# Mixing weights summed pair by pair, and five smaller moves around the attention-to-experts handover

## What is computed

```
x = x + xattn(layernorm(x), ctx, ctx)          # 16 heads of 16, rope, row q sees keys q-64 .. q
z = layernorm(x).reshape(1600, 256)
logits = z @ router_w.T                        # 8 experts
topk_p, topk_i = top_k(softmax(logits), 2); topk_p /= topk_p.sum(-1)
for e in range(8):
    sel = topk_i == e; mask = sel.any(-1)
    mean_w = (topk_p * sel).sum() / max(mask.sum(), 1)      # one number for each expert
    h = silu(z @ gate_w[e].T) * (z @ up_w[e].T)             # 1024 wide
    out += mask[:, None] * (h @ down_w[e].T) * mean_w
x = x + out
```

## Time and profile before

| | us |
|---|---|
| median of 3 runs (range) | 498.06 (497.79 to 502.31) |
| profiled execution | 498.84 |
| its span, first to last instruction | 497.0 |
| PE busy | 448.1 (90%) |
| DVE busy | 301.9 (61%) |
| ACT busy | 271.8 (55%) |
| POOL busy | 125.0 (25%) |
| mean granted TensorE clock | 0.962 |

### The profile page before, as it was taken

How to read it: one execution, slowest core, us unless ns; L and a number is a source line. 1 busy time by engine, 2 the same in 40 slices (tenths; PEclk the granted TensorE clock), 3 DMA queues, 4 the chain that set the end, 5 groups by cost and what they waited for, 6 DMA issues and landing times.

```text
span 497.0 us, 8914 instructions
## 1 busy us (share of the span) xinstructions
PE 448.1 (90%) x2788; PEld 371.4 (75%) x2788; DVE 301.9 (61%) x728; ACT 271.8 (55%) x855; POOL 125.0 (25%) x129
## 2 busy tenths in 40 slices
...
GB/s 236 30 245 119 167 23 42 30 65 8 63 10 59 21 47 52 56 241 226 176 191 54 162 155 135 176 103 164 154 131 171 103 169 125 37 31 39 9 2 36
...
## 3 DMA queue, kind: packets, MB, share of 16 engines
...
...
## 4 chain that ended last, share of the span: by engine, by line
PE 70%; ACT 8%; DVE 8%; issue 5%; POOL 3%; DMA 3%; SPq 2%; ACTq 1%; POOLq 0%; DVEq 0%
PE b_o L694 8%; PE b_small L694 8%; PE b_s L681 7%; PE b_s L683 7%; PE b_s L682 7%; PE b_s L442 6%; ACT probs L814 4%; PE b_pv L465 3%; PE b_pt L451 3%; PE b_proj L520 2%; PE b_pt L681 2%; PE b_pt L682 2%; PE b_pt L683 2%; PE b_s L440 2%; PE b_o L540 2%
## 5 line engine op out<-in xcount | busy, mean ns | idle before, releaser
L814 ACT ACTIVATE probs<-b_s,negmax 100x100 f32<-100x100 f32 x256 | 85.8, 361 | 21.9 <-DVE negmax L1092 18.9
L1302 POOL DMA_INDIRECT out<-y_sb,idnow x32 | 49.7, 1552 | 159.8 <-ACT y_sb L854 152.5
L842 ACT CAST h_hi<-h_sb 128x448 fp32r<-128x448 f32 x64 | 36.3, 567 | 87.6 <-DVE h_sb L1169 87.6
L681 PE MATMUL b_s<-x_hi,w_hi 128*128 128x448 f32 x192 | 72.0, 375 | 0.0
L683 PE MATMUL b_s<-x_hi,w_lo 128*128 128x448 f32 x192 | 70.9, 369 | 0.0
L682 PE MATMUL b_s<-x_lo,w_hi 128*128 128x448 f32 x192 | 70.6, 368 | 0.0
L1070 DVE TENSOR_TENSOR w_lo<-w_raw,w_hi 128x1024 fp32r<-128x1024 f32 x48 | 58.8, 1224 | 13.8 <-ACT w_hi L777 13.8
L1173 DVE TENSOR_TENSOR h_lo<-h_sb,h_hi 128x448 fp32r<-128x448 f32 x64 | 40.0, 625 | 40.5 <-ACT h_hi L842 40.5
L814 ACT ACTIVATION_READ_ACCUMULATOR probs<-b_s,negmax 100x1 f32 x256 | 56.8, 222 | 0.0
L442 PE MATMUL b_s<-kblk,qrot 128*100 128x400 f32 x128 | 53.6, 499 | 0.0
L1092 DVE TENSOR_REDUCE negmax<-b_s 100x4 f32<-100x400 f32 x64 | 36.2, 566 | 24.5 <-PE b_s L442 23.9
...
## 6 DMA issues: line engine op xcount, KB each, us to landing
...
kblk<-krot SPq DMA_DIRECT2D x128, 12.5 KB, 1.8
...
```

The lines of the kernel that those rows point to most:

```text
L681: pe.matmul(o, wh[:, c, cols], x_hi[:, c, :], start=(c == 0), stop=False)
L814: m = nc.scalar.activation(probs[:, N % 3, h, :], b_s[N % 3][0:S, h * S:(h + 1) * S], ACT.Exp, bias=negmax[:, N % 4, h:h + 1], accum_out=p ...
L842: nc.scalar.copy(h_hi[:, f, :], h_sb[:, f % 2, :]).then_inc(s_hhi, 1)
L1302: G.indirect_dma_start(out, bass.IndirectOffsetOnAxis(idnow[:, n:n + 1], 0), y_sb[:, n, :], None, bounds_check=TOK + TILE - 1, oob_is_err= ...
```

## The change

- `weight_sums` works on one pair: DVE's differences, ACT's exponentials and POOL's sums of pair i-2 are made in round i, and POOL adds them into `wacc`. On POOL the sums of pairs 6 and 7 stand ahead of the second half of `scatter(6)` and of `scatter(7)`; the first half of `scatter(6)` stands between them. PE waits for the eighth sum (`s_wpair`).
- The pad rows of tile 0 and the slot numbers are sent behind the key blocks of pair 2; the tail of expert e+1 is written one load earlier than before, and the tails count on two semaphores in turn.
- `early_tile` is made of transposes in place of plain products, and six `warm` matmuls are added around it and around `route_logits(6)`, with one more ahead of it.
- ACT applies SiLU to one number between `x_high(0)` and the reloads, so the table of SiLU is loaded there.
- `take_ids(0)` stands at step 3 (`FC - 5`) of tile 0 in place of step 5.

Left out of the diff: semaphores and buffers that are only renamed.

```diff
@@ -145,12 +145,13 @@
         topi = sb("topi", [S, 2, E], U32)
         choice = sb("choice", [S, TOPK, 2])
         sel = sb("sel", [S, NPAIR, TOPK * 2, E])
-        delta = sb("delta", [S, TOPK, B])
-        etop = sb("etop", [S, TOPK, B])
-        esum = sb("esum", [S, B])
-        erec = sb("erec", [S, B])
-        wtop = sb("wtop", [S, TOPK, B])
-        wsel = sb("wsel", [S, NPAIR, TOPK * 2, E])
+        delta = sb("delta", [S, 2, TOPK, 2])
+        etop = sb("etop", [S, 2, TOPK, 2])
+        esum = sb("esum", [S, 2])
+        erec = sb("erec", [S, 2])
+        wtop = sb("wtop", [S, TOPK, 2])
+        wsel = sb("wsel", [S, TOPK * 2, E])
+        whalf = sb("whalf", [S, 2, E])
         chosen = sb("chosen", [S, 2, E], BF16)
         before = sb("before", [S, 3, E], BF16)
         place = sb("place", [S, 2, E])
@@ -159,6 +160,7 @@
         desti = sb("desti", [S, 2, TOPK * 2], U32)
         wacc = sb("wacc", [S, E])
         credit = sb("credit", [1, 4])
+        table = sb("table", [1, 1])
 
         cnt = sb("cnt", [P, E])
         cnt1 = sb("cnt1", [P, E])
@@ -368,11 +369,12 @@
             sp.wait_ge(s_zero, 3)
             key_blocks(0)
             load_rows(2, 2, NPAIR)
-            sp.dma_start(slots[0:TILE, :], padrows).then_inc(s_pre, 16)
-            sp.dma_start(slot_sb[:, :], slotno).then_inc(s_slot, 16)
             for i in pairs:
                 if i + 1 < NPAIR:
                     key_blocks(i + 1)
+                if i == 1:
+                    sp.dma_start(slots[0:TILE, :], padrows).then_inc(s_pre, 16)
+                    sp.dma_start(slot_sb[:, :], slotno).then_inc(s_slot, 16)
                 if i >= 1:
                     store_x2(i - 1)
             for q in s_scat:
@@ -386,10 +388,11 @@
                 n = sp.value_load(counti[0:1, e:e + 1], min_val=0, max_val=TOK)
                 row = nc.s_assert_within(n + e * REGION, 0, E * REGION - TILE)
                 sp.dma_start(slots[bass.ds(row, TILE), :].rearrange("(p g) w -> p (g w)", g=GRP),
-                             padrows.rearrange("(p g) w -> p (g w)", g=GRP)).then_inc(s_tails, 16)
+                             padrows.rearrange("(p g) w -> p (g w)", g=GRP)).then_inc(s_tails[e % 2], 16)
 
             sp.wait_ge(s_tail, 1)
             write_tail(0)
+            write_tail(1)
             sp.wait_ge(s_first, 1)
             for e in range(E):
                 lo = sp.value_load(first[0:1, e:e + 1], min_val=0, max_val=MAXTILES)
@@ -398,7 +401,7 @@
                     for q in s_scat:
                         sp.wait_ge(q, 16 * TOPK * 2 * (NPAIR // 2))
                     sp.wait_ge(s_xt[DC - 1], 2)
-                sp.wait_ge(s_tails, 16 * (e + 1))
+                sp.wait_ge(s_tails[e % 2], 16 * (e // 2 + 1))
                 with sp.Fori(lo, hi) as t:
                     sp.wait_ge(s_xt[DC - 1], t + 1)
                     sp.wait_ge(s_id, t + 1)
@@ -406,8 +409,8 @@
                     sp.dma_start(xin[:, :, :].rearrange("p g w -> p (g w)"),
                                  slots[bass.ds(row, TILE), :].rearrange("(p g) w -> p (g w)", g=GRP)
                                  ).then_inc(s_in, 16)
-                if e + 1 < E:
-                    write_tail(e + 1)
+                if e + 2 < E:
+                    write_tail(e + 2)
             total = sp.value_load(first[0:1, E:E + 1], min_val=1, max_val=MAXTILES)
             taken = sp.to_reg(total + 1)
             sp.wait_ge(s_xt[DC - 1], taken)
@@ -585,7 +588,8 @@
                 for c in range(DC):
                     for g in range(GRP):
                         pe.matmul(b_xt[c][:, g * ROWS:(g + 1) * ROWS], xin[:, g, c * P:(c + 1) * P],
-                                  ident[0:ROWS, 0:ROWS], start=(g == 0), stop=False, skip_group_check=True)
+                                  ident[0:ROWS, 0:ROWS], is_transpose=True, start=(g == 0), stop=False,
+                                  skip_group_check=True)
 
             def late_rows(i):
                 last = i == NPAIR - 1
@@ -614,8 +618,9 @@
                     if cur:
                         scores(i, n)
                     if n == 5 and i == NPAIR:
-                        warm(4)
+                        warm(5)
                         early_tile()
+                        warm(3)
                     if n == 5 and 0 <= i - 2 < NPAIR:
                         ranks(i - 2)
                     if n == 2 and prv:
@@ -644,8 +649,12 @@
                         o_project(2 * i - 1)
                     if n % 4 in (0, 1) and 0 <= N - 3 < NQ * NPAIR:
                         values(N - 3)
+                    if n == 2 and i == NPAIR:
+                        warm(2)
                     if n == 2 and 0 <= i - 2 < NPAIR:
                         route_logits(i - 2)
+                    if n == 2 and i == NPAIR:
+                        warm(1)
                     if n == 2 and i == NPAIR + 1:
                         late_rows(NPAIR - 2)
 
@@ -656,7 +665,7 @@
                       start=True, stop=True).then_inc(s_cnt, 1)
             warm(4)
             late_rows(NPAIR - 1)
-            pe.wait_ge(s_wacc, 1)
+            pe.wait_ge(s_wpair, NPAIR)
             pe.matmul(b_o[:, 0:E], cst[0:S, C_ONE:C_ONE + P], wacc[:, :],
                       start=True, stop=True).then_inc(s_wsum, 1)
 
@@ -767,6 +776,12 @@
                 nc.scalar.copy(xn2T[:, :, :, :].rearrange("p b c s -> p (b c s)"),
                                b_small[:, 0:DC * PT]).then_inc(s_x2Tc, 1)
 
+            def top_exponentials(i):
+                a.wait_ge(s_dl, i + 1)
+                if i >= 2:
+                    a.wait_ge(s_wpair, i - 1)
+                nc.scalar.activation(etop[:, i % 2], delta[:, i % 2], ACT.Exp).then_inc(s_et, 1)
+
             def rows_high(i):
                 a.wait_ge(s_xr, i + 1)
                 nc.scalar.copy(xr_hi[:, i % 2], xrow[:, i % 2, :, 0:D]).then_inc(s_xrh, 1)
@@ -792,6 +807,8 @@
                             a.wait_ge(s_pv, M - 2)
                         nc.scalar.copy(probsT[:, M % 3].rearrange("p h s -> p (h s)"),
                                        b_pt[0:S, 0:QH * S]).then_inc(s_pTc, 1)
+                    if n == 5 and 0 <= i - 2 < NPAIR:
+                        top_exponentials(i - 2)
                     if n == 1 and i == NPAIR:
                         rows_high(NPAIR - 2)
                     if n == 0 and i == NPAIR + 1:
@@ -825,8 +842,6 @@
                         evac_proj(i + 1, 0, s_q, s_qc)
 
 
-            a.wait_ge(s_dl, 1)
-            nc.scalar.activation(etop[:, :, :], delta[:, :, :], ACT.Exp).then_inc(s_et, 1)
 
             def x_high(t):
                 for c in range(DC):
@@ -883,6 +898,7 @@
                     step(t, e, par, False, False)
 
             x_high(0)
+            nc.scalar.activation(table[:, :], cst[0:1, C_ONE:C_ONE + 1], ACT.Silu)
             for k in range(WCH):
                 reload(-1, k)
             a.wait_ge(s_first, 1)
@@ -1058,11 +1074,11 @@
                     V.tensor_tensor(onehot[:, b, :], slot_sb[:, :], bc(here[:, b:b + 1], [S, TILE]), ALU.is_equal
                                     ).then_inc(s_hot, 1)
 
-            def top_differences():
-                V.tensor_tensor(delta[:, :, :].rearrange("p k t -> p t k"),
-                                top[:, :, :, 0:TOPK].rearrange("p i b k -> p (i b) k"),
-                                bc(top[:, :, :, 0:1].rearrange("p i b k -> p (i b) k"), [S, B, TOPK]),
-                                ALU.subtract).then_inc(s_dl, 1)
+            def top_differences(i):
+                if i >= 2:
+                    v.wait_ge(s_et, i - 1)
+                V.tensor_tensor(delta[:, i % 2].rearrange("p k b -> p b k"), top[:, i, :, 0:TOPK],
+                                bc(top[:, i, :, 0:1], [S, 2, TOPK]), ALU.subtract).then_inc(s_dl, 1)
 
             def weights_low(e, par, k):
                 v.wait_ge(s_whi, WCH * (e + 1) + k + 1)
@@ -1115,8 +1131,8 @@
                         residual(i - 1)
                     if n == 3 and 0 <= i - 2 < NPAIR:
                         choose_counts(i - 2)
-                    if n == 3 and i == NPAIR + 1:
-                        top_differences()
+                    if n == 3 and 0 <= i - 2 < NPAIR:
+                        top_differences(i - 2)
                     if n == 4 and prv and i < NPAIR:
                         residual(i - 1)
                     if n == 5 and cur:
@@ -1179,7 +1195,7 @@
                     hidden_low(t, f)
                     if split and f < WCH:
                         weights_low(e, par, f)
-                    if e == 0 and split and f == FC - 3:
+                    if e == 0 and split and f == FC - 5:
                         take_ids(0)
                     if f == FC - 2:
                         v.wait_ge(s_idnow, t + 1)
@@ -1230,37 +1246,33 @@
                 ps[0] += 1
                 g.wait_ge(pool_self, ps[0])
 
-            def weight_sums():
-                g.wait_ge(s_et, 1)
```

(52 more changed lines are left out.)

7 lines of the change are left out of this document (3 added, 4 removed).

## The result

| | before | after |
|---|---|---|
| median (range, runs), us | 499.35 (497.79 to 502.31, 4) | 485.92 (483.92 to 487.85, 4) |
| ratio, 95% interval | | 0.972 [0.965, 0.980] |
| profiled execution; its span, us | 498.84; 497.0 | 483.92; 482.1 |
| mean granted TensorE clock | 0.962 | 0.982 |

Faster by 2.8%, and 6.3 us above the forecast of 479.6. Three later measurements of the unchanged file gave 487.87, 487.76 and 487.38 (ratios 0.973, 0.976, 0.975), so the result is about 487, and the profiled execution above is among the fastest that this kernel ran (the fastest took 483.82).

What follows compares the result with a forecast made beforehand. PE was taken to bound the kernel, with three reachable waits: handover, tile 1 and start. Terms -2.9 + 0.4 + 0 - 8.1 - 7.9 = -18.5 from 498.84 gave 480.3, forecast as median 479.6, range 476.5 to 485.5 us.

Steps and rivals of the forecast that it cites:

- attention: Attention rounds: pair-by-pair sums add work on DVE, ACT and POOL; +0.4 us taken, bounds 0 and +3.1.
- Routing: Routing of pairs 6 and 7, with transposes and seven more warm matmuls: 0 taken, bounds -1.5 and +0.5 us.
- D: Rival: POOL's sums delay each attention round, so the kernel is slower than before, 515 us; chance 0.02.
- E: Rival: the change doesn't do what it says, the two waits remain under other names, 490 to 495 us; chance 0.04.
- Start: PE's 2.93 us wait before pair 1's first scores goes as key blocks are issued earlier: -2.9 us, bounds 1.4 and 2.9.
- Step 0 at full clock: First step of the experts runs at full clock after the handover: -1.9 us, 0 if the clock is down.
- rival B: PE's clock stays at 0.50 through the handover, because of transposes or idle time; +4 to +5, 484 us; chance 0.18.
- Tile 1: Earlier take_ids(0) removes PE's wait for the second tile's load and the half clock behind it: -7.9 us.
- the margin of 0.8: Tile 0's row numbers were to land at 232.7, 0.8 us before take_ids(0) at step 3 wants them at 233.5.
- handover: Between late rows and experts, PE's wait for wacc goes: -7.0 for the start, -1.9 for step 0, +0.8; together -8.1 us.
- Rival C: Tile 0's row numbers come late, holding DVE and tile 1's load: +3.2 and clock +2.8, 485 us; chance 0.14.
- A: The forecast itself, 479.6 us; with its terms' bounds 476.5 to 484; chance 0.62.

Runs made afterwards that it cites:

- no_preload: The changed kernel without the early SiLU table load ahead of the reloads: 487.46 us, 0.974 of the kernel before.
- oldroute: The changed kernel with the early tile as plain products again and the seven added warm matmuls taken out: 488.31 us, 0.973 of the kernel before.
- pads_early: The changed kernel with pad rows and slot numbers sent where they were before: 490.46 us, 0.978 of the kernel before.
- few_bytes: The changed kernel with each of the six reloads moving an eighth of its piece: 485.50 us, 0.970 of the kernel before.
- few_warm: The changed kernel with each of the six reloads cut to an eighth, plus six more warm matmuls ahead of the experts: 484.22 us, 0.966 of the kernel before.
- before_ids3: The kernel before with take_ids(0) at step 3 alone: 492.30 us, 0.980 of the kernel before.
- again3: The changed kernel measured again unchanged, as partner for other runs on its chip: 487.38 us, 0.975 of the kernel before.
- warmfill: The changed kernel with six more warm matmuls in PE's pauses ahead of the experts: 486.64 us, 0.970 of the kernel before.

## Why the prediction was right and wrong

Against the profiled execution the sum said -18.5, and it was -14.9; by medians it said -18.5 and was about -13. Step by step, in span time before and after:

| up to | before | after | difference | forecast, cumulative |
|---|---|---|---|---|
| residual of pair 0 | 56.08 | 54.78 | -1.3 | -2.9 |
| residual of pair 6 | 187.90 | 186.84 | -1.1 | -2.5 |
| second `x_lo` | 216.50 | 214.56 | -1.9 | -2.5 |
| end of the warm matmuls | 223.07 | 215.45 | -7.6 | -9.5 |
| first `h_sb` | 227.39 | 219.57 | -7.8 | -9.7 |
| last `h_sb` of tile 0 | 258.65 | 243.77 | -14.9 | -18.5 |

**Right.** The three waits went, and where: PE ran from the late rows into the experts, and the load of tile 1 was issued at step 3 or 4. From the residual of pair 0 to that of pair 6 attention grew by 0.24 (+0.4 in the sum), though POOL had 11.67 busy in 25 us. The table load beside the reloads cost nothing and brought nothing (`no_preload`). Routing came to 0 (`oldroute`). Rivals D and E are out.

**Start, too large.** -2.9 taken, the lower bound of -1.4 was nearer: -1.3 in the profile, 2.0 by `pads_early`. SP did start the key blocks 0.02 behind the keys (29.71, the keys' operation ending at 29.69), where it had been 1.37. But the keys themselves ended 1.5 later in this execution than in that of before (29.69 for 28.18), which hides that much of it. PE's wait of 2.93 fell to 0.50 here, and to 0.7 to 1.8 in most other profiles with the pads moved: the key blocks still land a little late, more often than I had it.

**Step 0 at full clock, not got.** The forecast took -1.9 for it and had the experts start at full clock. The clock fell at 212.06, behind PE's pauses between 208.6 and 210.1 where it waits for pair 7's routing. So the warm matmuls and step 0 ran at half clock: this is rival B's mechanism in part of its place. The first `h_sb` started at 219.57, where the forecast, less what it took for the stages ahead, has 217.7: 1.9 later, 0.6 of it from the stages ahead and 1.3 from the clock. Without further warm matmuls the clock was down somewhere between 210 and 220 in all but one (`no_preload`) of the ten profiles of the changed kernel and its versions with transposes and the pads moved; with them it was up from 215 to 225 in five of five. But they did not keep it up: in four of these five it was down between 207 and 213 instead, where less hangs on it. In `oldroute`, with plain products and without the seven warm matmuls, it was down at 200 to 205 and up through the handover. The rule that I had weighed, that transposes do not count as PE work for the clock as other matmuls do (the Trainium skill, "TensorE: Matmul & The Clock Gate", Part 4), is not settled by this: the transposes of the early tile ran at 201 to 202 with the clock at 1.00 and it stayed there until 212, but `oldroute` changes the kind of matmul and the warm ones at once. In time the two versions don't differ.

**Tile 1, the step that failed.** "Load at 227.8, landed 4.9 later: 232.7, 0.8 in time." Those times are in the clock of before; less the 2.5 for the stages ahead, load 225.3, landed 230.2, tile 1 issued 231.7, landed 236.5. Measured: 227.94, 233.53, 234.62, 240.28, so 3.8 late, as much as the miss of the profiled execution, 3.6. In parts: the last scatter ended at 221.58 where the forecast has 220.1 on that scale (+1.5, of which 0.6 are stages ahead that gained less and 0.7 the sums of pair 7, 3.2 on POOL where I had 2.5); from there to the load it took 6.36, where I had 3.5 and 1.7 for more bytes (+1.2); the loads took 5.59 and 5.66, not 4.9 (+0.7 and +0.8); the rest went against the margin of 0.8 and the step from the numbers to the load (1.07 for 0.67). I had seen the full DMA and priced it by the bytes that the change adds (0.65 MB). The price is that of all bytes that now fall together: before, the issue of the reloads ended 6.6 us ahead of that of the last scatter (218.63 to 225.19), the DMA engines were still full when it went out and empty from 228 on; afterwards it ends 4.1 ahead, and the reloads of steps 1 and 2 (223.57 and 226.92), which came at 231.40 and later before, fall in as well, so that the engines stay full beyond 230. The change brought the scatters forward into the burst. `few_bytes` and `few_warm` show it: without most of the bytes of the six reloads the landing is 3.5 to 4.2.

The late chain was not the only path that was late. PE reached tile 1 at 239.57, where the forecast, on the same scale, has 236.8. Of the 3.6 of the miss 0.6 are stages ahead, 1.3 step 0 at half clock, 0.8 what DVE's wait for the row numbers and its copy added between steps 3 and 4, and 0.75 PE's wait for tile 1. So two terms failed, each by about 1.5, and the margin of 0.8 by which the row numbers were to be there turned into a wait of 0.52 to 1.50 on DVE in the four profiles of the unchanged file.

And it had a second error in it, one of structure. The terms "handover" and "tile 1" were added as if they were independent. By the ratios, the sums alone bring 3.2, `take_ids` alone 10.1, the pads 2.0: 15.3, and all together 12.8 (mean ratio 0.974). The intervals of the three add up to more than the 2.5 between them, so that this much is lost is argued, not shown. The profiles point the same way: from the residual of pair 0 to the end of the span the sums alone save 6.4, while all that the change adds to `before_ids3` (430.3) is 0.4 to 3.0, some of it hidden by that run's early step 0. In `before_ids3` PE comes at 247.17 and tile 1 is there; move PE forward as well and the chain of transfers is next, which doesn't move with it. Rival C was this chain, with the right place; I gave it 0.14, and its price (485; its own terms, +3.2 and +2.8, give 485.6) was close to what came, 487. Close by luck in part: in the profiled execution only 1.5 of the miss is this chain's. Its second half, the clock falling in that wait, came in five profiles with PE's wait at 1.75 to 3.27 (`pads_early`, `again3`, `oldroute`, `no_preload`, `warmfill`), and not in five with 0.75 to 1.95.

**From the profile to the median.** I took the 0.8 by which the median of before lay below its profiled execution for the changed kernel too. Here the profiled one was the fastest of 4, and four measurements have medians of 485.92 to 487.87. The residual of pair 0 began at 54.16 to 59.73 in the profiles with the pads moved, and from it to the end of the span the four of the unchanged file took 427.3 to 429.9 (before: 440.9): much of the spread lies in the start, ahead of anything that the handover touches; where in it, no run settles. By medians this is 2.8 of the miss of 6.3: 0.8 taken off, and 2.0 by which the median lay above the profiled execution.

The range ended at 485.5 and missed. A's bounds were not added up rightly either: they give 477.7 to 485.6, not 476.5 to 484. The range had the bounds of single terms, but B and C at once were in none, and part of both is what happened.
